# Causal attention on one Trainium2 core: masking a diagonal tile by a minimum on VectorE in place of triangle products on TensorE

## The reference

```
q, k, v = heads(Wq, bq), heads(Wk, bk), heads(Wv, bv)      # 16 heads of 8 channels
q, k = rope(q), rope(k)
att = einsum('bhqd,bhkd->bhqk', q, k) * (1.0 / sqrt(8))
att = where(tril(ones((T, T), bool)), att, NEG_BIG)
att = softmax(att, axis=-1)
y = einsum('bhqk,bhkd->bhqd', att, v)
return y @ Wp.T + bp
```

## Time and profile before

| | |
|---|---|
| median of 3 runs | 2931.68 us (2924.8 to 2933.88) |
| the profiled execution's own time | 2924.75 us |
| its span, first to last instruction | 2922.9 us |
| mean granted TensorE clock over the span | 0.863 of full speed |
| first and last triangle product in the scores (L1095) | 754.3 and 1119.1 us from the span's start |

### The profile page before, as it was taken

How to read it: one execution, slowest core, us unless ns; L and a number is a source line. 1 busy time by engine, 2 the same in 40 slices (tenths; PEclk the granted TensorE clock), 3 DMA queues, 4 the chain that set the end, 5 groups by cost and what they waited for, 6 DMA issues and landing times. The chain is left out here.

```text
span 2922.9 us, 48929 instructions
## 1 busy us (share of the span) xinstructions
PE 2228.8 (76%) x17406; PEld 1126.6 (39%) x17406; DVE 2015.4 (69%) x3638; ACT 1537.9 (53%) x3073; POOL 1227.9 (42%) x1268
## 2 busy tenths in 40 slices
PE   6999977876899995774836787777622976889886
PEld 2333333544444443553812333333222872233232
DVE  7888858886566663663248999999762227888884
ACT  4788861111566663331537666666321224767775
POOL 5423204433434220342445677677664444542310
PEclk9999997877999997776967888989956997999998
DMA  4121210000121212013930000000013971223110
GB/s 118 26 42 31 48 55 1 1 1 1 25 51 33 48 27 63 22 24 96 310 96 0 1 0 1 0 0 1 0 36 118 303 251 42 40 42 55 39 30 16
DMA packets 127625, 152.80 MB, mean 52 GB/s; under 512 B 19992, under 2 KB 108760, under 8 KB 126776
## 3 DMA queue, kind: packets, MB, share of 16 engines
q1 hardware_dynamic: 120792, 136.12, 17.3%
q0 software_dynamic: 6592, 13.56, 1.3%
HBM read 96.15 MB, written 25.59 MB: 42 GB/s over the span
## 5 line engine op out<-in xcount | busy, mean ns | idle before, releaser
L479 DVE TENSOR_REDUCE a_mx<-banks 128x2 f32<-128x1024 f32 (+3 forms) x768 | 806.1, 1087 | 236.5 <-PE banks L1051 127.2
L892 ACT ACTIVATE a_prob<-banks 128x512 f32<-128x512 f32 (+3 forms) x1536 | 744.9, 541 | 268.4 <-PE banks L1089 147.2
L1116 PE MATMUL banks<-a_prob,a_vaug 128*32 128x256 f32 (+2 forms) x5632 | 435.0, 390 | 0.2
L2216 POOL TENSOR_TENSOR m_hc<-m_h,m_cs 128x512 f32<-128x512 f32 x256 | 332.4, 1320 | 132.2 <-DVE m_h L2081 131.2
L1089 PE MATMUL banks<-a_Qs,a_Ks 64*128 64x512 bf16 (+3 forms) x1536 | 326.5, 366 | 44.7 <-DMA a_Qs<-a_negm 23.4
L2081 DVE TENSOR_TENSOR_SCAN m_h<-banks,m_u 128x512 f32<-128x512 f32 x256 | 300.9, 1208 | 21.1 <-issue 21.1
L1042 PE MATMUL banks<-a_Ks,a_Qs 63*128 63x512 bf16 (+3 forms) x1536 | 286.3, 369 | 35.0 <-DVE a_mx L479 28.2
L2364 PE MATMUL banks<-m_hc,kc 128*128 128x512 f32 x512 | 292.9, 657 | 9.6 <-DVE m_yf L2198 8.5
L2272 ACT ACTIVATE banks<-m_dt,acoef 128x512 f32<-128x512 f32 x256 | 174.9, 689 | 137.0 <-DVE m_h L2081 136.1
L1042 PEld LDWEIGHTS banks<-a_Ks,a_Qs 63*128 63x128 bf16 x1536 | 74.3, 93 | 330.6 <-issue 168.5
L1116 PEld LDWEIGHTS banks<-a_prob,a_vaug 128*32 128x32 f32 x5632 | 119.1, 109 | 157.7 <-issue 115.7
(11 more groups left out here) (429 smaller groups left out, 4237.5 us busy)
## 6 DMA issues: line engine op xcount, KB each, us to landing
c_wbuf<-in_w2e SPq DMA_DIRECT2D x71, 512.0 KB, 4.1
b_wbuf<-in_w1e SPq DMA_DIRECT2D x39, 578.0 KB, 4.6
a_Ks<-a_parts SPq DMA_DIRECT2D x252, 64.0 KB
a_Qs<-a_parts SPq DMA_DIRECT2D x252, 64.0 KB
rows_in<-in_unused SPq DMA_DIRECT2D x1, 4579.5 KB, 17.9
c_yb<-rows_in SPq DMA_DIRECT2D x71, 64.5 KB, 4.5
a_mixed_in<-rows_back SPq DMA_DIRECT2D x16, 256.0 KB, 4.3
a_Qs<-a_negm SPq DMA_DIRECT2D x192, 2.0 KB
```

What stands on the lines that cost most here:

```text
L479: dve.tensor_reduce(both[:, :, c], m_bank(u)[:, :, 0:keys[c % NT]], AX.X, ALU.max).then_inc(S("m_read"), 1)
L892: act.activation(prob[:, n % DEEP, first_query[kt]:T], s_bank(u)[:, first_query[kt]:T], ACT.Exp, scale=scale).then_inc(S("s_read"), 1)
L1116: i = pe.matmul(V[32 * hl:32 * hl + 32, q0:q1], vaug[:, b % 3, kt, g % NG * GH + hl, :], prob[:, (4 * a + hl) % DEEP, q0:q1], start=kt == ...
L2216: gp.tensor_tensor(hc[:, n % 6, :], h[:, n % 4, :], cs[:, k % 4, :], ALU.mult).then_inc(S("weighed"), 1)
```

## The change

The triangle products of the scores (not those of the maxima) are gone, with their tables. The exponentials above the diagonal of a diagonal tile are now computed without a mask and set to zero afterwards: VectorE takes the minimum of the exponentials of the four heads of a tile (128 x 4 x 128, in place in `prob`) and a table that holds 0 above the diagonal and 3e38 elsewhere. The values wait for this (`p_masked`) in place of the exponentials. Due times of the values move from 4a + 6.5 to 4a + 7.6, and those of the output turn, its copy, the output product and the store by 1.0 (`behind`). The other attentions are not touched.

```
+        "keep1": np.where(np.arange(P)[:, None] > np.arange(P)[None, :], 0.0, 3e38).astype(np.float32),
...
+                behind = 1.0 if causal else 0.0
-                m_at.update({("oturn", g): 32 * g + 38.2 for g in range(NGB // 2)})
+                m_at.update({("oturn", g): 32 * g + 38.2 + behind for g in range(NGB // 2)})
-                m_at.update({("out", b): 64 * b + 78.2 for b in range(B)})
+                m_at.update({("out", b): 64 * b + 78.2 + behind for b in range(B)})
-                s_at.update({("oback", b): 64 * b + 74.7 for b in range(B)})
+                s_at.update({("oback", b): 64 * b + 74.7 + behind for b in range(B)})
...
+                def vector_mask(dve):
+                    for a in range(16 * B):
+                        q0 = first_query[a % NT]
+                        yield 4 * a + 5.2
+                        s_done(dve, ("score", 4 * a + 3))
+                        own = prob[:, 4 * a % DEEP:4 * a % DEEP + 4, q0:q0 + P]
+                        dve.tensor_tensor(own, own, keep.unsqueeze(1).broadcast_to([P, 4, P]),
+                                         ALU.min).then_inc(S("p_masked"), 1)
...
-                        yield 32 * g + 36.0
+                        yield 32 * g + 36.0 + behind
...
-                        yield 64 * b + 82.0
+                        yield 64 * b + 82.0 + behind
...
-                            i = pe.matmul(s_bank(u)[:, q0:T], Ks[lo:lo + HALF, b % 4, pair, kt * P:(kt + 1) * P],
-                                          Qs[lo:lo + HALF, b % 4, pair, q0:T], start=True, stop=not causal)
-                            if not causal:
-                                i.then_inc(S("s_written"), 1)
-                        if causal:
-                            for par in range(2):
-                                pe.matmul(s_bank(("score", n + par))[:, q0:q0 + HALF], tri_table("scoreL0", HALF * par),
-                                          tri_table("scoreR0", HALF * par), start=False, stop=False)
-                            for par in range(2):
-                                pe.matmul(s_bank(("score", n + par))[:, q0 + HALF:q0 + P], tri_table("scoreL1", HALF * par),
-                                          tri_table("scoreR1", HALF * par), start=False, stop=True).then_inc(S("s_written"), 1)
+                            pe.matmul(s_bank(u)[:, q0:T], Ks[lo:lo + HALF, b % 4, pair, kt * P:(kt + 1) * P],
+                                      Qs[lo:lo + HALF, b % 4, pair, q0:T], start=True, stop=True).then_inc(S("s_written"), 1)
...
-                            yield 4 * a + 6.5 + half * (0.05 if kt == NT - 1 else 2.0)
+                            yield 4 * a + (7.6 if causal else 6.5) + half * (0.05 if kt == NT - 1 else 2.0)
                             if half == 0:
-                                s_done(pe, ("score", 4 * a + 3))
+                                if causal:
+                                    pe.wait_ge(S("p_masked"), a + 1)
+                                else:
+                                    s_done(pe, ("score", 4 * a + 3))
```

More of the change, by code:

```diff
@@ L75 @@
 PACK_KB = [("identb", 128), ("block", 512), ("prefix", 128), ("ones", 128), ("sel32", 32), ("sel16", 1024),
-           ("maxL0", 128), ("maxL1", 128), ("scoreL0", 128), ("scoreL1", 128),
-           ("cornQ", 512), ("cornK", 512), ("maxR0", 64), ("maxR1", 64), ("scoreR0", 64), ("scoreR1", 64),
+           ("maxL0", 128), ("maxL1", 128), ("cornQ", 512), ("cornK", 512), ("maxR0", 64), ("maxR1", 64),
            ("cornL", 128)]
@@ L345, in rep, with attention_all @@
             return piece.unsqueeze(1).broadcast_to([P, NT, C])
-        def attention_all(tag, xres, w, scale, causal=False, corners=False, swapped=None, double=None, bo=None,
+        def attention_all(tag, xres, w, scale, causal=False, keep=None, corners=False, swapped=None, double=None, bo=None,
                           load=None, store=None, mixed=None, gated=None):
@@ L1168, in attention_all @@
                            "sync": sync_batch, "tensor": tensor_batch}
+                if causal:
+                    lanes["vector"].append(vector_mask)
                 if mixed:
@@ L1405, in build @@
             attention_all("a1_", xres, (wa("wq1"), wa("wk1"), wa("wv1"), wa("wp1"), c1[:, 0:1], c1[:, 1:2], wa("bv1")),
-                          scale, causal=True,
+                          scale, causal=True, keep=wa("keep1"),
                           swapped=(wa("wqs1"), wa("wks1"), c1[:, 2:3], c1[:, 3:4], wa("cos1"), wa("sin1")),
@@ L2640, in triangles @@
     later = np.where(r[None, :] > r[:, None], NEG, 0.0)
-    left = {name: np.zeros((n, P)) for name in ("maxL0", "maxL1", "scoreL0", "scoreL1")}
+    left = {name: np.zeros((n, P)) for name in ("maxL0", "maxL1")}
     corner = {"cornQ": np.zeros((n, T)), "cornK": np.zeros((n, T))}
@@ L2644, in triangles @@
     corner["cornK"][0, T - 1] = corner["cornK"][1, 0] = NEG
-    right = {"maxR0": later.copy(), "maxR1": later.copy(), "scoreR0": later.T.copy(), "scoreR1": later.T.copy()}
+    right = {"maxR0": later.copy(), "maxR1": later.copy()}
     left["maxL0"][r, r] = 1
@@ L2649, in triangles @@
     right["maxR1"][n - 1] = NEG
[L2650 to L2653, removed]
     table = np.concatenate([*left.values(), *corner.values(), *right.values()], 1)
```

## The result

| | before | after |
|---|---|---|
| median of 6 runs (range), us | 2929.3 (2924.8 to 2933.9) | 2957.5 (2955.6 to 2966.9) |
| profiled execution, its span, us | 2924.75, 2922.9 | 2957.09, 2955.3 |
| ratio, 95% interval | | 1.0099 (1.0083 to 1.0115) |

A forecast was written before the change was run, and what follows sets the result against it. A loop over TensorE, GpSimd and SyncE's queue bounds each batch, so TensorE's savings count only ahead of ks. 6 x (5.7 - 0.36 - 0.5) = 29, plus 4: +33 on 2924.75, 2958; on the median 2965, stated 2964, range 2930 to 2988.

The forecast's parts named there:

- one more step on VectorE: Values and maxima wait for the mask's own latency on VectorE: 1.2 us a batch up to the second maxima.
- shared path: VectorE's two-input SBUF minimum and GpSimd's operations exclude each other for about their length; called the large term.
- saving ahead of ks: On TensorE before the last projection: 0.36 us from removed triangles and 0.5 from a moved values piece, a batch.
- late second maxima: The second group's maxima reach SyncE's queue 5.7 us late a batch, delaying all sends behind them.
- The masks wait for GpSimd: Masks beside GpSimd's rotations and subtraction wait 5.1 us in sum a batch; this main forecast had chance 0.62.
- Removed triangles: Score products dropped from TensorE save 0.06 us a pair, counted for six pairs ahead of ks: 0.36 us a batch.
- Part 4: From the second maxima's DMA to TensorE's next start after its DMA wait: queue needs 17.28 us, nothing added.
- The clock: TensorE's half clock after the DMA wait costs 2.2 us a batch; change taken as zero, bound 13 us either side.
- Tail: Six last groups without sends: 4.25 of them have maxima, at 0.9 us each, 4 us lost.
- Rival B: Faster: values have slack, masks fit VectorE's idle time, TensorE's time is the stage's: 18 us less, 2914; chance 0.11.
- Rival A: Hidden: masks find GpSimd free or wait only a little; +6 us, 2938, no change that can be told; chance 0.17.
- Rival C: Worse: clock falls before the second maxima (+13), masks wait up to 2.36 us each (+11 counted): 2988; chance 0.10.

The follow-up runs named there:

- x2: Changed kernel without the minima, values waiting for the exponentials alone, so the mask inside the diagonal tiles is left out: 0.9974 of the kernel before.
- x1: Changed kernel with a one-input reduction over the same elements in place of each minimum, masking left out: 1.0013 of the kernel before.
- y5: Changed kernel with GpSimd's three rotations and two subtractions of a batch each cut into two halves: 1.0079 of the kernel before.
- z3: Changed kernel with masks due ahead of the reductions and GpSimd's rotations and subtractions in halves: 0.9997 of the kernel before.
- z4: Kernel before with the negated maxima's DMAs issued by ScalarE in place of SyncE, in the causal stage alone: 0.9982 of the kernel before.
- x4: Kernel before with the triangle products of the scores left out and nothing else changed, no minimum: 0.9993 of the kernel before.

## Why the prediction was right, step by step

In shares of about 2930 us, the chain x2, x1, after splits the change into three, each beside its term of the prediction (each measured difference is uncertain by some 6 us):

| | predicted | measured |
|---|---|---|
| triangles and order, no mask | 6 x -0.86 = -5 | 0.9974: -8 |
| one more step on VectorE, no shared path | 6 x 1.2 + 4 = +11 | 0.9974 to 1.0013: +11 |
| shared path | 6 x 4.5 = +27 | 1.0013 to 1.0099: +25 |
| sum | +33 | +29 |

The same in the profile, by stretches of the stage. The prediction's saving ahead of ks (0.86 a batch) falls in the first to the sixth loop; its late second maxima (5.7) fall in the second to the seventh, for the first loop has its sends ahead of the masks. So the sixth late maxima lie behind the seventh rotation.

| from rotation to rotation | predicted | measured |
|---|---|---|
| first to second | -0.9 | 48.9 to 50.9: +2.0 |
| second to seventh, five loops | 5 x 4.84 = +24 | 239.5 to 259.4: +19.9 |
| seventh to the last exponentials | 5.7 + 4 = +10 | 87.7 to 92.0: +4.3 |
| sum | +33 | +26 |

The two profiled executions differ by 32.3 us. 7.0 of it lie behind the stage (from its last exponentials to the end 1803.5 before, 1810.5 after); the runs from x1 to y5, z3 and z4 have 1807.2 to 1814.7 there, so it looks like the one execution of before that was profiled, which was short there, and not like the change. The medians differ by 28.

- **The masks wait for GpSimd: right in kind, a fifth too dear.** The replay gave six masks a batch 5.1 us of waiting, the first 2.0. In the batch shown each mask's length less 0.68 is 1.96, 0, 0.69, 0.37, 0.59 and, for the sixth, 0: 3.6 in all; over all 128 masks it is 24.6 us, 4.1 for each of six batches. GpSimd's first part was to be 1.65 us later; its cast ends 9.4 us behind the start of the rotation in place of 8.2, 1.2 later. The second maxima's DMA came 4.4 us later in this batch and 4.6 in the mean of the five, in place of 5.7; x1 shows 0.8 of it without the shared path (predicted 1.2). The Trainium skill's page "SBUF — State Buffer", section "Who interferes with whom", has it that the pair of ports is locked for the whole instruction, and that on this chip a tensor_reduce never takes it; the trace agrees with both, 1.96 us of waiting for the minimum and 689 ns as the longest of 128 reductions.
- **Removed triangles: right as far as it can be told.** TensorE's saving is swallowed where the DMA wait stands: x4's grew by 8.5 us, and x4's whole time, 0.9981 to 1.0004, leaves no room for the 15 us that would go if TensorE's own time were the stage's.
- **Part 4, nothing added: wrong by 1.4 us a batch.** The DMA wait went as said (19.0 to 3.7 us, of which 3.3 lie ahead of the second rotation), but from the second maxima to the next q the five loops take 23.39 us in place of 21.95 in the mean. x1, whose reductions never wait for GpSimd, has 23.46 there and x2, without any mask, 21.70: what is added comes with one more step on VectorE, of which I had let the queue hide all. A stretch of half clock lies there too, in x1 as in the changed kernel; how much is the step's latency and how much the clock is not separated.
- **The clock, taken as zero: it moved.** In the five loops the stretch from q to ks takes 6.77 us in place of 8.81 in the mean, 2.04 less, of which I had 0.86. The pair of q took 2.07 or 2.08 us in five of the six batches of before, as at 973.65, and takes 1.12 or 1.13 in four of six after, as at 886.99. The granted clock there was 0.50, 1.2 GHz; it is 1.00, 2.4 GHz, in this window of the changed kernel:

```profile
887.00:888.00 1.00, 1.00 (x2) 0.29 (x2) 0.00 (x0) 0.39 (x2) 0.00 (x0) 1.00 0.00 0
```

  But the half clock is not gone from the stage, whose mean went from 0.93 to 0.92. It falls on the way to the second maxima now, as the prediction feared ("the clock may fall there"), and in part 4. What it costs there is inside the 4.6 and the 1.4 us above and was not measured apart. An estimate from the windows of 1 us in the batch shown (clock 0.94, 0.50, 0.50, 0.50, 0.86 from 903 on): 3.4 us at half clock on the way to the second maxima, of which the full clock could save at most half, 1.7 us.
- **Luck.** Three errors share the five loops: part 4 +1.4, ahead of ks -1.2, the lateness -1.1 a batch. The first two nearly cancel, and what is left, 3.97 us a batch against 4.84, is mostly the size of the lateness. Nothing in the prediction foresaw that they cancel.
- **Tail: its 4 us did not show.** 92.0 - 87.7 = 4.3 us looks like the predicted 4, but the stretch holds the sixth late second maxima (21.51 us behind ks in place of 17.46, +4.1). From there to the last exponentials it is 72.2 us before and 72.4 after. With 2 or 3 us of noise in a tail the term of 4 is not excluded, but nothing shows it.
- **What would show it.** L1095 and L1098 of before are gone, the shortest mask is 0.675 us, 28 of 128 are longer than 0.7 (six of them 2.63 or 2.64), GpSimd's rotations grow by up to 0.46 us (I had written up to 0.7), and the loops are 51 to 53 us long from the second on.
- **Rival B** fell with x2: without any mask, 18 us don't come. **Rival A** would have been right for an operation with one input: x1 stands at +4 us, predicted +6. **Rival C** came by half: the clock does fall in part 3, in five of six batches, but it rises around q in most, and no mask waited more than 1.96 us. The 2988 didn't come.

## What to carry to other kernels

Before work is moved from TensorE to VectorE, ask which engine leads at that moment and whether the new instruction reads two SBUF operands while GpSimd runs: here, against no mask at all, the same elements with one operand cost 11 us and with two 36, in a stage where VectorE had 150 us to spare. If both engines must run, cut GpSimd's operations short and put VectorE's ahead of what it can wait with: together these took the loss away here, each alone only a part. And when TensorE waits for a DMA, look at how many DMAs the issuing queue carries before you look at their order: the one reordering that was tried moved the 19 us to another line, and taking eight a batch away from the queue made the kernel a little faster (0.9982). When a wait goes and the half clock behind it, look for where the half clock stands now before you book the gain.

## What I had not expected of the hardware

- Two edits that gave 10 and 6 us gave 30 together (the 14 us beyond their sum are uncertain by 11).
- GpSimd lost less in a meeting than the mask is long: 2.81 - 2.35 = 0.46 us for a mask of 0.68, which ended 0.60 us behind the start of that rotation.
- The half clock moved with the waits. Behind TensorE's DMA wait it went in four of six batches; in the batch shown it came back behind idle times of TensorE of 0.3 to 1.1 us that masks and maxima caused, where no DMA was waited for. The q at 937.85 of the changed kernel took 1.96 us with no DMA wait ahead of it in that batch.
- ScalarE pays 1.28 us for two DMA issues, and its next exponential starts 1.36 us after the copy.
